# A four-layer transformer on one core: the last attention's steps in another order, and two projections split into bfloat16 parts from PSUM

## What is computed

```python
# layer 0: q0, q1, k0, k1, v = x @ w (16 heads of 8), differential attention
# layer 1: q, k, v = x @ W + b (16 heads of 8); queries kept by max minus mean of their scores
# layer 3, 16 heads of 64:
q, k, v = x @ Wq, x @ Wk, x @ Wv          # [b, h, t, 64]
logits = (q @ k.T + causal + rel_pos_bias) / 64
probs = softmax(logits)
out = (probs @ v).reshape(b, t, h * 64) @ Wo + bo
```

## Time and profile before

| | us |
|---|---|
| median of 3 runs (3791.26 to 3796.87) | 3793.6 |
| the profiled execution | 3826.92 |
| its span, first to last instruction | 3825.1 |
| first projection (layer 0), 37.0 to 129.5 | 92.5 |
| second projection (layer 1), 1095.5 to 1170.0 | 74.5 |
| last attention (layer 3), 2952 to 3743 | 791 |

### The profile page before, as it was taken

How to read it: one execution, slowest core, us unless ns; L and a number is a source line. 1 busy time by engine, 2 the same in 40 slices (tenths; PEclk the granted TensorE clock), 3 DMA queues, 4 the chain that set the end, 5 groups by cost and what they waited for, 6 DMA issues and landing times. The chain is left out here.

```text
span 3825.1 us, 87256 instructions
## 1 busy us (share of the span) xinstructions
PE 3345.6 (87%) x26852; PEld 2091.7 (55%) x26852; DVE 2373.0 (62%) x6059; ACT 2026.3 (53%) x4169; POOL 1563.8 (41%) x2652
## 2 busy tenths in 40 slices
PE   4799999999967999859999867979874999999997
PEld 2344444777632222237777523679762666666664
DVE  5688887323346888667777755178356565666564
ACT  5588888443354888813333343333344666666662
POOL 0266667000011233227777626055571444444440
PEclk9799999999966999979999878878696999999999
DMA  5423322000022121145665211300033333333330
GB/s 135 105 70 76 74 72 63 22 6 12 4 74 63 48 47 44 26 93 156 162 159 158 77 64 37 104 6 3 13 59 73 102 117 117 117 117 117 117 97 23
DMA packets 200113, 289.70 MB, mean 76 GB/s; under 512 B 41100, under 2 KB 157004, under 8 KB 199520
## 3 DMA queue, kind: packets, MB, share of 16 engines
q1 hardware_dynamic: 195748, 277.81, 26.7%
q0 software_dynamic: 4096, 8.40, 1.4%
HBM read 234.81 MB, written 35.93 MB: 71 GB/s over the span
## 5 line engine op out<-in xcount | busy, mean ns | idle before, releaser
L779 ACT ACTIVATE att_E<-att_pX,att_gs 128x512 f32<-128x512 f32 x1152 | 718.0, 683 | 133.0 <-PE att_pX L708 132.3
L1957 POOL TENSOR_TENSOR att_E<-att_E,att_rz 128x128 f32<-128x128 f32 (+3 forms) x512 | 357.4, 719 | 436.1 <-DVE att_rz L2167 436.1
L834 DVE TENSOR_REDUCE att_mx<-att_pS 128x2 f32<-128x1024 f32 (+2 forms) x448 | 434.7, 992 | 86.7 <-PE att_pS L686 71.9
L686 PE MATMUL att_pS<-arr_ks,arr_qs 72*128 72x512 bf16 (+4 forms) x1536 | 423.0, 339 | 50.7 <-DVE att_mx L834 27.6
L708 PE MATMUL att_pX<-arr_qs,arr_ks 75*128 75x512 bf16 (+4 forms) x1536 | 420.8, 329 | 8.9 <-DMA arr_qs<-att_mp 4.8
L1697 POOL TENSOR_TENSOR pairs_h<-pairs_m,pairs_r 128x512 f32<-128x512 f32 x272 | 345.6, 1271 | 194.0 <-DVE pairs_m L1760 129.1
L1721 PEld LDWEIGHTS pairs_po<-pairs_a,pairs_h 128*128 128x128 f32 x2176 | 286.5, 192 | 130.4 <-issue 129.2
L826 DVE CUSTOM_DVE_ANT_0 att_seen<-att_pS,arr_later 128x384 bf16<-128x384 f32 (+1 forms) x512 | 298.8, 613 | 80.4 <-PE att_pS L686 80.0
L1742 ACT ACTIVATE pairs_r<-pairs_ph 128x512 f32<-128x512 f32 x272 | 162.4, 597 | 330.1 <-PE pairs_ph L1713 328.9
L721 PE MATMUL att_pO<-att_E,att_vs 128*9 128x512 f32 (+3 forms) x3072 | 298.5, 491 | 9.2 <-ACT att_E L779 8.7
L2099 ACT ACTIVATE att_E<-att_S,att_nm 128x128 f32<-128x128 f32 (+3 forms) x512 | 283.0, 557 | 40.3 <-DVE att_nm L2161 40.1
(11 more groups left out here) (413 smaller groups left out, 6458.9 us busy)
## 6 DMA issues: line engine op xcount, KB each, us to landing
pairs_c<-weights SPq DMA_DIRECT2D x272, 256.0 KB, 3.9
att_bias<-in_bias_dram SPq DMA_DIRECT2D x64, 896.0 KB, 5.1
parts<-proj_part SPq DMA_DIRECT2D x144, 128.0 KB, 2.3
att_xb<-xnT SPq DMA_DIRECT2D x64, 256.0 KB, 5.4
arr_qs<-parts SPq DMA_DIRECT2D x192, 64.0 KB
arr_ks<-parts SPq DMA_DIRECT2D x192, 64.0 KB
att_w<-in_w3a_dram SPq DMA_DIRECT2D x64, 192.0 KB, 5.1
arr_qs<-parts SPq DMA_DIRECT2D x96, 96.0 KB
```

The source lines that it names most:

```text
L686: ins = nc.tensor.matmul(pS[:, bank, n * w:(n + 1) * w], qs[:K1, u, x, q * P:(q + 1) * P], ks[:K1, u, x, :w], start=(n == 0 or not causal) ...
L779: nc.scalar.activation(E[:, c % NE], pX[:, BANK2[(g * NP2 + c) % (NB * NP2)]], ACT.Exp, scale=gs[:, g % 2, gain_of:gain_of + 1]).then_inc( ...
L834: V.reduce_max(dst, src, AX.X).then_inc(s_mx, 1)
L1957: nc.gpsimd.tensor_tensor(E[:, k, :width(j)], E[:, k, :width(j)], rz[:, u, k:k + 1].broadcast_to([P, width(j)]), ALU.mult).then_inc(s_n, 1)
```

## The change

In the projections VectorE takes `rest` straight from PSUM (product times scale, or plus bias, minus `part[0]`), so the float32 copy `full` goes away; ScalarE makes the middle part from `rest`, and VectorE the low part from that. Middle and low part of a tile are done one tile later than its high part. Semaphores take the place of the drains. In layer 0 `ps` has four places and `part` eight; in layer 1 two and four. There the sum of the keys is taken from PSUM, and the bias is added to it as 512 times the bias.

In the last attention the value projection stands ahead of the weighted sums in step 0 on TensorE, and its copy ahead of the output copy on ScalarE; the values have four places instead of two; on VectorE the minimum passes of a step stand ahead of its inverse.

```diff
@@ project_phase
-        full = p.sb("full", [P, 2, T])
-        rest = p.sb("rest", [P, 2, T])
-        part = p.sb("part", [P, 4, 3, T], BF16)
+        PR, PW = (4, 8) if mean is None else (2, 4)
+        rest = p.sb("rest", [P, 4, T])
+        part = p.sb("part", [P, PW, 3, T], BF16)
...
-        ps = p.ps("ps", [P, 2, T])
+        ps = p.ps("ps", [P, PR, T])
@@ project_phase, ScalarE
+                def middle(at, g):
+                    act.wait_ge(s_rest, at(2 * M2, g + 1))
+                    nc.scalar.activation(part[:, g % PW, 1], rest[:, g % 4], ACT.Copy).then_inc(s_mid, 1)
...
-                            for dst in (full[:, g % 2], part[:, g % 4, 0]):
-                                ins = nc.scalar.activation(dst, ps[:, g % 2], ACT.Identity, bias=bias[:, m:m + 1],
-                                                           scale=qsc[:, 0:1] if qscale and m % 2 == 0 else 1.0)
-                            ins.then_inc(s_full, 1)
+                            nc.scalar.activation(part[:, g % PW, 0], ps[:, g % PR], ACT.Identity, bias=bias[:, m:m + 1],
+                                                 scale=qsc[:, 0:1] if qscale and m % 2 == 0 else 1.0).then_inc(s_hi, 1)
+                            if not (first and g == 0):
+                                middle(at, g - 1)
...
+                    if last:
+                        middle(at, 2 * M2 - 1)
@@ project_phase, VectorE
+                def low(at, g):
+                    dve.wait_ge(s_mid, at(2 * M2, g + 1))
+                    dve.nop(nofuse=True)
+                    nc.vector.tensor_tensor(part[:, g % PW, 2], rest[:, g % 4], part[:, g % PW, 1], ALU.subtract).then_inc(s_split, 1)
...
-                            nc.vector.tensor_tensor(r1, x, pt[:, 0], ALU.subtract)
                             if mean is not None and m == 1:
-                                nc.vector.reduce_sum(kbar[:, u], x, AX.X)
-                            dve.drain()
+                                nc.vector.reduce_sum(ksum[:, u], ps[:, g % PR], AX.X).then_inc(s_ks, 1)
+                            factor = mean is None
+                            nc.vector.scalar_tensor_tensor(out=rest[:, g % 4], in0=ps[:, g % PR],
...
+                            if not (first and g == 0):
+                                low(at, g - 1)
...
-                            nc.vector.tensor_copy(pt[:, 1], r1)
-                            dve.drain()
-
-                            nc.vector.tensor_tensor(pt[:, 2], r1, pt[:, 1], ALU.subtract).then_inc(s_split, 1)
+                    if last:
+                        low(at, 2 * M2 - 1)
@@ layer3_attention
-        v = p.sb("v", [P, 2, QT, P])
+        v = p.sb("v", [P, VR, QT, P])
@@ layer3_attention, TensorE
+                        if j == 0 and not (last and m + 1 >= PAIRS):
+                            project(at, 2, m + 1, first)
                         if j % 2 == 0:
...
-                        if j == 0 and not (last and m + 1 >= PAIRS):
-                            project(at, 2, m + 1, first)
@@ layer3_attention, ScalarE
+                        if j == 0 and not (last and m + 1 >= PAIRS):
+                            leave(at, 2, m + 1, first)
                         if j == 0 and not (first and m == 0):
                             outputs(at, m - 1, first and m == 1)
-                        if j == 0 and not (last and m + 1 >= PAIRS):
-                            leave(at, 2, m + 1, first)
@@ layer3_attention, VectorE
-                        if not (last and s + 2 >= STEPS):
-                            invert(at, s + 2, first)
                         if not (last and s + AHEAD >= STEPS):
                             extreme(at, 2 * (s + AHEAD), first)
                             extreme(at, 2 * (s + AHEAD) + 1, first)
+                        if not (last and s + 2 >= STEPS):
+                            invert(at, s + 2, first)
```

More of the change, by code:

```diff
@@ L324, in project_phase @@
         s_mm = p.sem("mm")
-        s_full = p.sem("full")
+        s_hi, s_rest, s_mid = p.sem("hi"), p.sem("rest"), p.sem("mid")
         s_split = p.sem("split")
-        s_put = [p.sem(f"put{k}") for k in range(4)]
+        s_put = [p.sem(f"put{k}") for k in range(PW)]
         s_vmm = p.sem("vmm")
@@ L375, in body @@
                             g = u * M2 + m
-                            if not (first and g < 2):
-                                pe.wait_ge(s_full, at(2 * M2, g - 1))
-                            nc.tensor.matmul(ps[:, g % 2], w[:, m], xb, start=True, stop=True).then_inc(s_mm, 1)
+                            if not (first and g < PR):
+                                pe.wait_ge(s_rest, at(2 * M2, g + 1 - PR))
+                            nc.tensor.matmul(ps[:, g % PR], w[:, m], xb, start=True, stop=True).then_inc(s_mm, 1)
                         if not (first and u == 0):
                             pe.wait_ge(s_vT, at(2, u))
-                        nc.tensor.matmul(pv[:, 0], w[:, M2], xb, start=True, stop=True).then_inc(s_vmm, 1)
+                        nc.tensor.matmul(pv[:, :], w[:, M2], xb, start=True, stop=True).then_inc(s_vmm, 1)
                         pe.wait_ge(s_vT, at(2, u + 1))
@@ L442, in body @@
                             g = u * M2 + m
-                            x, r1 = full[:, g % 2], rest[:, g % 2]
-                            pt = part[:, g % 4]
-                            dve.wait_ge(s_full, at(2 * M2, g + 1))
+                            dve.wait_ge(s_hi, at(2 * M2, g + 1))
                             if not (first and g < 4):
-                                dve.wait_ge(s_put[g % 4], at(M2 * 24, 48 * (g // 4)))
-                            nc.vector.tensor_tensor(r1, x, pt[:, 0], ALU.subtract)
+                                dve.wait_ge(s_split, at(2 * M2, g - 3))
                             if mean is not None and m == 1:
-                                nc.vector.reduce_sum(kbar[:, u], x, AX.X)
-                            dve.drain()
+                                nc.vector.reduce_sum(ksum[:, u], ps[:, g % PR], AX.X).then_inc(s_ks, 1)
+                            factor = mean is None
+                            nc.vector.scalar_tensor_tensor(out=rest[:, g % 4], in0=ps[:, g % PR],
+                                                           scalar=(qsc[:, 0:1] if qscale and m % 2 == 0 else 1.0) if factor else bias[:, m:m + 1],
+                                                           in1=part[:, g % PW, 0], op0=ALU.mult if factor else ALU.add, op1=ALU.subtract).then_inc(s_rest, 1)
+                            if mean is not None and m == 1:
+                                dve.wait_ge(s_ks, at(4, 2 * u + 1))
+                                nc.vector.scalar_tensor_tensor(out=kbar[:, u], in0=bias[:, 1:2], scalar=float(T), in1=ksum[:, u], op0=ALU.mult, op1=ALU.add).then_inc(s_ks, 1)
+                            if not (first and g == 0):
+                                low(at, g - 1)
                             if mean is not None and m == 1:
@@ L2083, in leave @@
                     act.wait_ge(s_pr, at(3 * PAIRS, 3 * m + k + 1))
[L2084 to L2089, removed]
-                    dst = (qT[:, u], kT[:, u], v[:, u].rearrange("p q f -> p (q f)"))[k]
+                    if k < 2 and not (first and m < 2):
+                        act.wait_ge(s_sc, at(STEPS, QT * (m - 1)))
+                    if k == 2 and not (first and m < VR):
+                        act.wait_ge(s_o, at(STEPS, QT * (m - VR + 1)))
+                    dst = (qT[:, u], kT[:, u], v[:, m % VR].rearrange("p q f -> p (q f)"))[k]
                     nc.scalar.activation(dst, pA[:, :], ACT.Copy).then_inc(s_pc, 1)
```

25 lines of the change are left out of this document (13 added, 12 removed).

## The result

The changed kernel takes **3869.75 us** (median of 4 runs, 3865.42 to 3876.99), the kernel before 3792.43 beside it: a ratio of **1.0204** (95% interval 1.0185 to 1.0222), 77 us slower. The forecast was 3876 in 3840 to 3910. The profiled execution of after has a span of 3863.7 us.

A forecast was written before the change was run, and what follows sets the result against it. TensorE was taken to bound the last attention, while neither TensorE nor VectorE filled the first projection. On the profiled 3826.9 us, +89 -6 -1 gave 3909; carried to the median, 3793.6 + 82 = 3876 us, range 3840 to 3910.

The forecast's parts named there:

- The pair of the last attention: Last attention: each pair of heads ends 1.41 us later, at 13.47 us; over 63 pairs +89 us.
- chain from scores to second transposes: Last attention: scores, minimum passes, reciprocal of row 2, divides, then the second head's transposes of row 2: 4.49 us.
- TensorE's move alone: Last attention: value projection ahead of the weighted sums, nothing else moved, removes a 0.5 us wait; gain 0.15 us per pair.
- VectorE's move alone: Last attention: reciprocal of row 2 behind row 3's minimum passes costs nothing by itself; 4.49 us against 4.51 before.
- The first rival: Last attention: divides not late if their chain takes under 2.9 us; pair 11.91 us, total 3778 us; chance 0.10.
- The first projection: First projection: eight places remove ScalarE's wait for transfers, SP's issue then bounds; gain 0 to 10.3 us, taken as -6.
- One sign: First projection, profile after: ScalarE would show no wait for transfers.
- The second projection: Second projection: a shorter way to the masked mean against a later end; -3.6 to +1.2 us, taken as -1.
- The counted pieces: Second projection: ScalarE's first copy to masked mean 4.6 us instead of 5.29; over eight items 0.8 to 5.6 us gained.
- The tail: Second projection's end: last middle part behind ScalarE's copy of the means, so the last low part starts some 2 us later.
- The sum: Whole kernel: +89, -6 and -1 us on the profiled execution, difference carried to the median: 3876 us; chance 0.80.
- The clock rival: Last attention: idle pieces in each pair drop TensorE's clock to 0.78; pair 15.1 to 17 us, total about 4040; chance 0.06.

The follow-up runs named there:

- the version with the reciprocal first: The changed kernel with the last attention's reciprocals back ahead of the two minimum passes, value projection still ahead of the weighted sums: 3774.9 us.

## Why the prediction was right, step by step

**The pair of the last attention.** Forecast 13.47 us, measured 13.40. Value projection at 1.88, measured 1.79; scores at 4.64, measured 4.55; chain from scores to second transposes 4.49, measured 4.46; transposes at 9.13, measured 9.01. The waits came where they were placed: 1.07 us for GpSimd, the one for the value copy gone, the reciprocal of row 2 without a wait for exponentials. The one shift is the handover after the key copy, counted as 0.14 and in fact some 0.1 shorter, so the wait there is 0.26 by the starts (1.79 against 1.53) and not 0.35. Forecast +89, measured +86.7 with the attention alone.

**Neither move alone.** The prediction gave TensorE's move alone -0.15 us a pair; measured 11.90 against 12.05, 3774.9 against 3786.1. It gave VectorE's move alone nothing; measured 12.06. One step under the -0.15 is not in its rows: it starts the transposes of row 2 0.88 us after the output projection (6.36 to 7.24), where the earlier trace rows have 0.97, which would have left a gain of 0.06. Measured are 0.89 (3307.63 to 3308.52 in the version with the reciprocal first), so this number came out right without a reason in the rows. The first rival rests on it; the sum of the forecast does not. The first rival (3778, divides not late) is what the kernel with the reciprocal first does; in the change its condition, a chain under 2.9 us, isn't met.

**The first projection.** Forecast -6 in 0 to -10.3; measured -8.0. The stage took 92.0 to 94.6 us in the three traces of the old form and 82.9 to 84.3 in the eight with the new one as in the change. Mis-sized was the part of SP's wait that goes: I took 6 of 10.3, and 9.2 went, since the faster split of the two engines keeps ahead of SP nearly throughout. One sign did not come: ScalarE was to be without a wait for transfers and has 4.3 us of it. Those waits no longer hold SP, whose own is 1.1.

**The second projection.** Forecast -1; measured -4.6 to +2.3 in the whole time. The counted pieces held. One item in after:

```profile
1106.32 0.69 ACT L418 ACTIVATE proj_qf<-proj_ps,pre_bias 128x512 f32<-128x512 f32 x1 [0.82 <-PE proj_ps L380]
...
1110.90 0.23 DVE L472 TENSOR_SCALAR proj_kblk<-pre_hmask,proj_kbar 128x16 f32<-128x16 f32 x1
...
1113.26 0.69 ACT L418 ACTIVATE proj_qf<-proj_ps,pre_bias 128x512 f32<-128x512 f32 x1 [0.63 <-PE proj_ps L380]
```

From first copy to mean 4.58 us, counted 4.6 (5.1 to 5.3 before). Over the eight items that is 35.9 us against 41.3, a gain of 5.4, the upper end of the 0.8 to 5.6 counted. The tail came too, and it is the mis-sized term: from the last mean to the stage's end 11.1 us (1146.61 to 1157.7) against 6.0 before, 5.1 more where the prediction had some 2. The rows show two things in it:

```profile
1146.81 0.42 SPq L307 DMA_DIRECT2D arr_qs<-parts  x1
...
1148.40 0.22 ACT L434 ACTIVATE total<-proj_pm 128x64 f32<-128x64 f32 x1 [1.45 <-PE proj_pm L396]
1148.53 0.62 ACT L407 ACTIVATE proj_part<-proj_rest 128x512 bf16<-128x512 f32 x1
...
1149.25 0.69 DVE L447 TENSOR_TENSOR proj_part<-proj_rest,proj_part 128x512 bf16<-128x512 f32 x1 [2.41 <-ACT proj_part L407]
...
1151.05 3.79 SPq L362 DMA_DIRECT2D parts<-proj_part  x6
```

The last middle part stands behind the copy of the means, as said. But the last low part is finished at 1149.94, and SP starts its three transfers, the second half of the six, only at 1152.93. What they stand behind is SP's ten loads for the next stage, 1146.81 to 1151.05, and the tile before; this the prediction had not counted. The same loads started 0.76 us ahead of the last item's first copy before (1159.05 and 1159.81) and start 4.69 behind it now, because they follow the transfers of the item before, whose last part is now made one tile later. So in this trace it is SP's queue that ends the stage, and not the late middle part; no run took either away.

What the sum left out is the stretch from the mean to the next first copy, which goes with TensorE's clock: 2.35 to 2.52 us wherever the clock granted in it was 1.00, 4.11 to 4.34 where it was 0.50, the lower level. Its seven lengths add up to 26.8, 25.2 and 23.5 us in the three traces with the old form, and to 17.8 to 22.7 (mean 20.0) in ten with the new one. The rest of the stage is 48.6 to 48.7 us in the old form and 48.1 to 48.7 in the new: a gain of 0.4, near the forecast -1, but as the difference of 5.4 and 5.1, so luck had a part in it. So the stage itself is some 5 us shorter, by the clock; the whole time of the kernel with the second projection alone doesn't show it. What gives it back, if anything does, is open.

**The sum.** 3876 was 6 too high: by the medians 2 in the attention and 4 in the projections (-7 forecast, -11.1 measured). How much of the 4 is real is open: the interval ends at -7.6, and one at a time the projections give -8.0 and +0.7. Carrying the difference over from an execution 33 us above the median was right: its excess is not in the last attention, whose stage is 794.0 to 795.9 us in the six later traces with a pair of 12.05 to 12.06 us. **The clock rival** (4040) did not come: with 1.07 us of idle pieces in every pair the granted clock of 3000 to 3700 in after stayed at 1.00, the higher level. What the Trainium skill (TensorE: Matmul & The Clock Gate, A second HAM failure mode) says of short idling between groups of matmuls does not show in this pattern.

## What to carry to other kernels

An instruction with its operands ready, put behind one that waits, inherits that wait: follow who waits for it, to the end. Two reorderings that are each harmless can lose together, when one makes an event later and the other hangs a chain on that event; measure S, the chain's length and the time at which its user arrives, and take the sum. Before a wait is removed by moving work ahead, try the slot just behind the work that doesn't need the resource: here that place, with the reciprocal first, beat both kernels.

## What the runs showed of the hardware

The clock granted in the second projection differs from execution to execution for the same instructions. Averaged over the seven stretches from a mean to the next first copy it was 0.58, 0.63 and 0.68 in the three traces of the old form and 0.70 to 0.93 in the ten of the new one; over the whole stage the two forms overlap (0.70 to 0.75 and 0.73 to 0.84). Why the form matters is open. That the old form holds the clock at the lower level is not so: in the kernel with the first projection alone two of its seven stretches stood at 1.00, with 2.52 and 2.36 us.

SP's 96 transfers of the first projection take 0.55 us each at the least, but in after they start over 73.6 us (42.6 to 116.2). One gap of 4.87 us holds the ten loads for the next stage; the other starts are 0.73 apart, with only 1.1 us of waiting in all. So the register work and the gaps between transfers count, and SP's own pace sets this stage.
